# One-core graph layer with residual and layer norm: the last two batches' x weighed at the outset, pairs packed from the second batch on, three transpose banks, two units' x added on TensorE, new end orders

## Chip, core and metric

The kernel runs on one core of one Trainium2 chip. The metric is the device time of one execution in microseconds; lower is better. The profile is of one execution by the hardware profiler. Engines: PE is TensorE (PEld its weight loads), DVE VectorE, ACT ScalarE, POOL GpSimd, SP SyncE.

## What is computed

```python
masks = (relation[None] == rel_ids[:, None, None, None]).astype(x.dtype)  # adj == 1..4
h = jnp.einsum('rbnm,bmd->rbnd', masks, x)        # B=8, N=1024, D=128, R=4
y = jnp.einsum('rbnd,rdo->bno', h, weight) + bias
out = layernorm(x + y, axis=-1)
```

The adjacency matrices (int32, 4 MB for each of 8 batches) hold only 0 and 1 in the inputs, so only relation 1 contributes. The kernel computes for that case, checks on the chip that it holds and that x is in range, and has a second pass for any other input, which is not entered here.

## The kernel before

A *unit* is 128 rows of an adjacency matrix (u = 0 to 7 in a batch), a *pair* is two units (k = 0 to 3), numbered through as 4b + k, so the last is pair 31. A pair is one load of 1 MB (the units of batch 0 come alone, 512 KB each). Output rows are handled in *groups* of four units, two to a batch (numbers 0 to 13); the last batch has five, of 2, 2, 2, 1 and 1 units, called a, a2, c, e, d.

What happens to a pair:

- SP loads it (`load_adj`, L405). Three slots; a slot is loaded again when pair 4b + k - 12 was checked. SP's queue is one order written out by hand: the units of batch 0, x of batch 1, then for each batch its pairs and x of the next. The stores come after all loads. ACT's queue issues x of batches 0 and 7 and the bias at the start.
- ACT checks it (`check`, L532): one pass over the pair that also writes it as bytes, two units side by side in 16 bits.
- PE transposes it. Packed (from pair 8 on, `transpose_pair`, L644) both units go in 8 transposes of the checked bytes; unpacked (L635) each unit takes 8 from the raw words, and waits for no check. Four PSUM banks (`T_BANKS`) take turns.
- DVE makes a mask out of each unit (`mask_unit`, L836). In the last batch ACT makes the masks of units 5 and 7 (`mask_second`, L578).
- PE multiplies (`products`, L666): 16 matmuls of 256 columns for two units, with x as a high and a low fp16 part. After four units ACT copies the sum (`copy_h`, L549), PE multiplies by the weight (`project`, L678), DVE adds x and bias (`sum_rows`, L843), takes statistics (L849) and combines them (L860).

The last batch is done the other way round. Its x is multiplied by the weight at the outset (transposed L688, kept by DVE L816, weighed L697, split into z_hi and z_lo by ACT L570 and DVE L821). `rows_of_unit` (L718) then gives a unit's rows in 16 matmuls of 128 columns with no copy and no projection. For the very last unit d, PE adds x as well (`add_x`, L728), so that DVE needs no sum.

The roots of a batch: ACT takes a square root (`root`, L554), DVE offers its reciprocal (`offer_guess`, L870), POOL makes of it scale and shift in seven small steps (`roots`, L470 to L487) and normalises unit by unit (L498). POOL also splits x of batches 2 to 6 (L444, L450) and adds the bias to every x (`add_bias`, L459). At the end three sets remain: `full` (batch 6), `ra` (units 0 to 3 of batch 7), `rb` (units 4 to 7). POOL normalises four units of `full`, two of `ra` and one of `rb`, in this order; ACT has the others but two; DVE has the last two (L899), whose scale it works out itself (L875 to L894). SP stores each set.

```python
            full, ra, rb = sets[B - 2:]
            roots(full)
            normalise(full, full.units[:4])
            roots(ra)
            normalise(ra, ra.units[:2])
            normalise(rb, rb.units[:1])
```

Of the kernel before, what the change touches and what calls it, by code (L numbers as in the profile page):

```python
# [5 lines left out]
P = 128  # L6
# [44 lines left out]
def adj_resnorm_kernel(nc, x, adj, weight, bias, out):  # L51
# [8 lines left out]
    FIRST_PACKED = 8  # L60
    T_BANKS = 4
# [29 lines left out]
    LAST = len(groups) - 5  # L91

# [42 lines left out]
    def pairs_checked_by(g):  # L135

        first = [3, 5, 8, 10]
        if g.index < len(first):
            return first[g.index]
        return min(2 * g.index + 4, PAIRS * B - 2)  # L140

    ctx = ExitStack()
    with ctx:
# [30 lines left out]
        z_hi = sb("z_hi", [P, J, D], FP16)  # L174
        z_lo = sb("z_lo", [P, J, D], FP16)
# [4 lines left out]
        x_t = h_all[:, 2:4, :]  # L180
# [20 lines left out]
        y_ps = pb("y_ps", [P, GU, D], FP32)  # L201

# [5 lines left out]
        def y_of(g):  # L208

            if g.index < LAST:  # L210
                return y_ps
            if g.place < 2:
                return h_ps[g.place][:, :].rearrange("p (n d) -> p n d", d=D)
            if g.place == 2:
                return y_ps
            if g.place == 3:
                return ids_t[0][:, :, :].bitcast(FP32).rearrange("p j q -> p (j q)").rearrange("p (n d) -> p n d", d=D)
            return spare

        def half_of_z(half):  # L220

            return (spare[:, :, :], h_ps[1][:, :].rearrange("p (n d) -> p n d", d=D))[half]
# [24 lines left out]
        s_turned, s_kept = sem("halves_of_last_x_transposed"), sem("halves_of_last_x_t_kept")  # L247
# [35 lines left out]
        x_v, adj_v, out_v = (t.rearrange("b (k p) d -> b p k d", p=P) for t in (x, adj, out))  # L283

# [104 lines left out]
        def _(sp):  # L389
# [42 lines left out]
        def _(pool):  # L432
# [20 lines left out]
            def add_bias(b):  # L453

                if b == B - 1:
                    pool.wait_ge(s_turned, 2)
                else:
                    pool.wait_ge(s_lo, b + 1)
                nc.gpsimd.tensor_tensor(x_sb[:, b], x_sb[:, b],  # L459
                                        bias_sb[:, :].unsqueeze(1).to_broadcast([P, J, D]),  # L460
                                        ALU.add).then_inc(s_xb, 1)

# [40 lines left out]
            add_bias(0)  # L503
            for b in range(B - 1):
                if b + 1 < B - 1:
                    if b:
                        split_hi(b + 1)
                    split_lo(b + 1)
                add_bias(b + 1)
# [12 lines left out]
        def _(act):  # L522
# [24 lines left out]
            def copy_h(g):  # L547
                act.wait_ge(s_prod, g.index + 1)
                nc.scalar.activation(h_all[:, g.bank, 0:g.count * P], h_ps[g.bank][:, 0:g.count * P], ACT.Copy,  # L549
                                     scale=0.5).then_inc(s_h, 1)  # L550
# [17 lines left out]
            def split_z(half):  # L568
                act.wait_ge(s_z, half + 1)
                nc.scalar.activation(z_hi[:, half * HALF:(half + 1) * HALF], half_of_z(half), ACT.Copy,  # L570
                                     scale=0.5).then_inc(s_zh, 1)

            def mask_second(u):


                act.wait_ge(s_mask, unit_no(B - 1, u) if u < J - 1 else unit_no(B - 1, u) - 1)
# [5 lines left out]
            act.dma_start(bias_row[:, :], bias.rearrange("(a d) -> a d", a=1)).then_inc(s_bias, 16)  # L582
            act.preload_act_table(ACT.Sqrt)
# [7 lines left out]
            split_z(0)  # L591
            check(0, 2)
            split_z(1)
            for g in groups[1:LAST]:
                copy_h(groups[g.index - 1])
# [24 lines left out]
        def _(pe):  # L620
# [26 lines left out]
            def products(g, units, part):  # L647

                if part is x_hi:
# [5 lines left out]
                    if g.index == 1 and units[0] == g.first:  # L655

                        pe.wait_ge(s_zl, 2)
# [13 lines left out]
            def project(g):  # L671
                pe.wait_ge(s_h, g.index + 1)
                if g.index == 0:
                    pe.wait_ge(s_biased, 1)
# [8 lines left out]
            def transpose_last_x(half):  # L683
                if half == 0:
                    pe.wait_ge(s_whole, 1)
                    pe.wait_ge(s_x[B - 1], 16)
                for n in range(HALF):
                    last = nc.tensor.transpose(half_of_z(half)[:, n, :], x_sb[:, B - 1, half * HALF + n, :],  # L688
                                               whole_ident[:, :])
                last.then_inc(s_turned, 1)  # L690

            def weigh_last_x(half):
                pe.wait_ge(s_kept, half + 1)
                if half == 0:
                    pe.wait_ge(s_w, 16)
                for n in range(HALF):
                    last = nc.tensor.matmul(half_of_z(half)[:, n, :], x_t[:, half, n * P:(n + 1) * P], w_sb[:, 0, :],  # L697
# [3 lines left out]
            def rows_of_unit(g, u):  # L701
                if u == g.first and g.place < 2:

                    pe.wait_ge(s_h, LAST - 1 + g.place)
                if u == g.first and g.place == 2:

                    pe.wait_ge(s_sum, LAST)
                pe.wait_ge(s_zl, 2)
                if g.place < 2 or g.place == 2 and u == g.first:
                    pe.wait_ge(s_mask, unit_no(g.b, u) + 1)  # L710
                elif g.place == 3:

                    pe.wait_ge(s_mask, unit_no(g.b, u))
                else:
                    pe.wait_ge(s_high, 1 if g.place == 2 else 2)
                for j in range(J):
                    for part in (z_hi, z_lo):
                        last = nc.tensor.matmul(y_of(g)[:, u - g.first, :], mask_t[:, g.b % 2, j, u * P:(u + 1) * P],  # L718
                                                part[:, j, :], start=(j == 0 and part is z_hi and g.place < 4),
# [4 lines left out]
            def add_x(g):  # L724

                pe.wait_ge(s_zl, 2)
                pe.wait_ge(s_xb, g.b + 1)
# [9 lines left out]
            idle_turns(44, 1)  # L737
# [24 lines left out]

            def step_by_two(g, units, b, k):
                if packed(b, k):
                    transpose_pair(b, k)
                    for part in (x_hi, x_lo):
                        products(g, units, part)
                elif (b, k) == (1, 0):

                    products(g, units, x_hi)  # L770
                    transpose_unit(b, 2 * k)
                    products(g, units, x_lo)
                    transpose_unit(b, 2 * k + 1)
                else:
# [3 lines left out]
                    products(g, units, x_lo)  # L778

            for g in groups[1:LAST]:  # L780
# [23 lines left out]
        def _(dve):  # L804
# [9 lines left out]
            def keep_last_x(half):  # L814
                dve.wait_ge(s_turned, half + 1)
                nc.vector.tensor_copy(x_t[:, half, :].rearrange("p (n d) -> p n d", d=D), half_of_z(half)).then_inc(s_kept, 1)  # L816

            def split_z(half):
                dve.wait_ge(s_zh, half + 1)
                js = slice(half * HALF, (half + 1) * HALF)  # L820
                nc.vector.scalar_tensor_tensor(out=z_lo[:, js], in0=half_of_z(half), scalar=0.5, in1=z_hi[:, js],  # L821
                                               op0=ALU.mult, op1=ALU.subtract).then_inc(s_zl, 1)

            def row_maxima_of_z():
                dve.wait_ge(s_zh, 2)
                nc.vector.tensor_reduce(row_max[:, B - 1, :], z_hi[:, :, :], AX.X, ALU.max,
# [13 lines left out]
            def sum_rows(g):  # L840
                dve.wait_ge(s_y, g.index + 1)
                dve.wait_ge(s_xb, g.b + 1)
# [64 lines left out]
            def find_far():  # L907

                dve.wait_ge(s_rm, B - 1)
                dve.wait_ge(s_zm, 1)  # L910
# [28 lines left out]
            keep_last_x(0)  # L939
            keep_last_x(1)  # L940
            for u in range(2, GU + 1):
                mask_unit(0, u)
            split_z(0)
            row_maxima(0)
            mask_unit(0, GU + 1)
            split_z(1)

            for g in groups[1:LAST]:
# [5 lines left out]
                if g.place == 0:  # L954
                    row_maxima(g.b)
                elif g.b:
# [3 lines left out]
                sum_rows(q)  # L960
                mask_unit(n.b, n.units[0])
# [4 lines left out]
                if g.index == 2:  # L966
                    row_maxima_of_z()
# [29 lines left out]
            normalise(rb, e.first, rows[:, rb.b, e.first, :])  # L997
# [21 lines left out]
```

## Time and profile before

| what | before |
|---|---|
| time, median of 3 runs | 110.03 us (109.78 to 110.26) |
| the profiled execution | 109.81 us, of which the span from first to last instruction is 108.0 |
| busy | PE 92%, PEld 86%, DVE 78%, ACT 79%, POOL 68% |
| moved by DMA | 42.21 MB, 391 GB/s over the span |
| granted clock | 0.989 of full |

A row of a timeline gives the start, the duration, the engine, the line and the tiles; in brackets, how long the engine was idle before it and what released it. Matmul ends are modelled, so for PE the starts are the surer figures.

### The profile page before, as it was taken

The page shows a single profiled execution, that of the slowest core. Times are in us where ns is not written, and L with a number is a line of the kernel's source. Part 1 is how long each engine was busy: PE and PEld are TensorE (multiplying, and loading weights), DVE is VectorE, ACT ScalarE, POOL GpSimd, SP SyncE. Part 2 cuts the span into 40 slices and gives each one's busy share as a digit, 9 for nine tenths or more (in the row PEclk, how much of TensorE's full clock was granted, in tenths as well). Part 3 has the DMA queues.
Part 4 walks back from the last instruction along what each step waited for, and adds up shares of the span by engine and source line. Part 5 has one row for each costly group of instructions (what it writes and reads, how often), then busy time and mean ns, then how long its engine had stood idle before and what let it go on. Part 6 is the DMA issues. An engine that isn't in the chain of part 4 may idle for free.

```text
span 108.0 us, 3036 instructions
## 1 busy us (share of the span) xinstructions
PE 99.9 (92%) x1100; PEld 92.4 (86%) x1100; DVE 83.9 (78%) x251; ACT 85.4 (79%) x103; POOL 73.6 (68%) x137
## 2 busy tenths in 40 slices
PE   5979999998999999999999999999999999999800
PEld 5957998998999999889998999899998999999800
DVE  1035779357979999699979998889978997997880
ACT  1346977979969897899799979997899879895850
POOL 3000800096099799989998899989998994934870
PEclk9999999999999999999999999999999999999995
DMA  3999999999999999999999999999999999999145
GB/s 58 350 414 420 420 414 435 431 428 403 437 428 431 411 419 432 428 422 414 429 431 428 413 422 434 434 422 419 422 428 425 428 419 426 414 419 367 58 201 199
DMA packets 7793, 42.21 MB, mean 391 GB/s; under 512 B 865, under 2 KB 994, under 8 KB 4194
## 3 DMA queue, kind: packets, MB, share of 16 engines
q1 hardware_dynamic: 7488, 40.96, 91.6%
q10 hardware_dynamic: 290, 1.05, 2.5%
q8 instruction: 9, 0.15, 0.5%
q14 instruction: 6, 0.05, 0.1%
HBM read 37.81 MB, written 4.19 MB: 389 GB/s over the span
## 4 chain that ended last, share of the span: by engine, by line
DMA 52%; PE 33%; DVE 7%; ACT 4%; issue 1%; DVEq 0%
DMA adj_sb<-adj 52%; PE h_ps L666 14%; PE ids_t L635 5%; PE y_ps L678 4%; PE ids_t L644 3%; PE h_ps L718 3%; ACT bytes_of L532 2%; DVE mask_t L836 2%; DVE x_lo L904 1%; ACT mask_t L578 1%; PE h_ps L697 1%; PE spare L697 1%; DVE stats L849 1%; PE spare L688 1%; DVE x_sb L899 1%
## 5 line engine op out<-in xcount | busy, mean ns | idle before, releaser
L532 ACT ACTIVATE bytes_of<-adj_sb,offset 128x2048 fp8e4<-128x2048 int32 x32 | 64.1, 2003 | 4.3 <-DMA adj_sb<-adj 3.8
L836 DVE TENSOR_SCALAR mask_t<-ids_t 128x1024 uint16<-128x1024 uint16 x62 | 40.4, 683 | 13.1 <-PE ids_t L635 11.1
L666 PE MATMUL h_ps<-mask_t,x_hi 128*128 128x256 bf16 (+1 forms) x232 | 29.2, 269 | 1.0 <-DVE mask_t L836 0.9
L666 PE MATMUL h_ps<-mask_t,x_lo 128*128 128x256 bf16 (+1 forms) x232 | 29.4, 269 | 0.2 <-DVE x_lo L904 0.2
L459 POOL TENSOR_TENSOR x_sb<-x_sb,bias_sb 128x1024 f32<-128x1024 f32 x8 | 19.1, 2382 | 9.9 <-ACT bias_sb L589 9.5
L498 POOL TENSOR_SCALAR x_sb<-x_sb,rstd,shift 128x128 f32<-128x128 f32 x55 | 23.9, 455 | 1.4 <-DVE shift L894 0.5
L666 PEld LDWEIGHTS h_ps<-mask_t,x_lo 128*128 128x128 f16 x232 | 21.9, 98 | 2.8 <-DVE x_lo L904 0.4
L666 PEld LDWEIGHTS h_ps<-mask_t,x_hi 128*128 128x128 f16 x232 | 21.1, 98 | 3.4 <-DVE mask_t L836 1.3
L450 POOL TENSOR_TENSOR x_lo<-x_sb,x_hi 128x1024 f16<-128x1024 f32 x6 | 12.9, 2146 | 8.3 <-ACT x_hi L545 7.9
L644 PE MATMUL ids_t<-ident,bytes_of 128*128 128x128 bf16 x192 | 16.2, 227 | 0.1
L644 PEld LDWEIGHTS ids_t<-ident,bytes_of 128*128 128x128 bf16 x192 | 14.6, 148 | 1.5 <-ACT bytes_of L532 1.1
L678 PE MATMUL y_ps<-w_sb,h_all 128*128 128x128 f32 x112 | 14.9, 276 | 0.0
L549 ACT ACTIVATE h_all<-h_ps 128x512 f32<-128x512 f32 x14 | 8.4, 599 | 7.1 <-PE h_ps L666 6.8
L849 DVE BATCH_NORM_STATS2 stats<-x_sb 128x6 f32<-128x128 f32 x63 | 13.8, 280 | 0.1
L678 PEld LDWEIGHTS y_ps<-w_sb,h_all 128*128 128x128 f32 x112 | 13.6, 192 | 0.3
L843 DVE TENSOR_TENSOR x_sb<-y_ps,x_sb 128x512 f32<-128x512 f32 (+1 forms) x15 | 9.9, 660 | 2.2 <-PE y_ps L678 2.2
L635 PE MATMUL ids_t<-ident,adj_sb 128*128 128x128 bf16 x128 | 10.6, 228 | 0.2 <-DMA adj_sb<-adj 0.2
L635 PEld LDWEIGHTS ids_t<-ident,adj_sb 128*128 128x128 bf16 x128 | 9.9, 148 | 0.5 <-issue 0.4
L811 DVE TENSOR_REDUCE row_max<-x_hi 128x8 f32<-128x1024 f16 x7 | 8.5, 1210 | 0.0
L444 POOL CAST x_hi<-x_sb 128x1024 f16<-128x1024 f32 x5 | 5.2, 1042 | 3.7 <-DMA x_sb<-x 3.7
L733 PE MATMUL h_ps<-mask_t 128*128 128x128 bf16 (+2 forms) x46 | 5.5, 311 | 1.2 <-DVE mask_t L928 1.2
L532 ACT ACTIVATION_READ_ACCUMULATOR bytes_of<-adj_sb,offset 128x1 f32 x32 | 6.0, 187 | 0.0
(85 smaller groups left out, 84.1 us busy)
## 6 DMA issues: line engine op xcount, KB each, us to landing
adj_sb<-adj SPq DMA_DIRECT2D x28, 1024.0 KB, 24.3
adj_sb<-adj SPq DMA_DIRECT2D x8, 512.0 KB, 8.7
out<-x_sb SPq DMA_DIRECT2D x7, 512.0 KB, 21.7
x_sb<-x SPq DMA_DIRECT2D x6, 512.0 KB, 23.4
x_sb<-x ACTq DMA_DIRECT2D x2, 512.0 KB, 6.5
out<-x_sb SPq DMA_DIRECT2D x2, 256.0 KB, 2.1
w_sb<-weight SPq DMA_DIRECT2D x1, 64.0 KB, 5.9
bias_row<-bias ACTq DMA_DIRECT2D x1, 0.5 KB
```

The costliest lines, as they stand in the source:

```text
L450: nc.gpsimd.tensor_tensor(x_lo[:, b % 2], x_sb[:, b], x_hi[:, b % 2], ALU.subtract).then_inc(s_lo, 1)
L459: nc.gpsimd.tensor_tensor(x_sb[:, b], x_sb[:, b], bias_sb[:, :].unsqueeze(1).to_broadcast([P, J, D]), ALU.add).then_inc(s_xb, 1)
L498: last = nc.gpsimd.tensor_scalar(rows[:, slot, u, :], rows[:, slot, u, :], rstd[:, slot, u:u + 1], shift[:, slot, u:u + 1], ALU.mult, ALU.add)
L532: nc.scalar.activation(bytes_of[:, at % ROOM].rearrange("p n t -> p t n"), adj_sb[:, slot, 2 * k:2 * k + 2, :], ACT.Square, scale=SLOPE, b ...
L635: last = nc.tensor.transpose(bank[:, j, :], words[:, j // step(b), j % step(b), 0, :], ident[:, :])
L644: last = nc.tensor.transpose(bank[:, j, :], words[:, j // step(b), j % step(b), :], ident[:, :])
L666: last = nc.tensor.matmul(h_ps[g.bank][:, to], part[:, g.b % 2, j, :], mask_t[:, g.b % 2, j, cols], start=(j == 0 and part is x_hi), stop= ...
L678: last = nc.tensor.matmul(y_of(g)[:, n, :], h_all[:, g.bank, n * P:(n + 1) * P], w_sb[:, 0, :], start=True, stop=True)
L811: nc.vector.tensor_reduce(row_max[:, b, :], x_hi[:, b % 2], AX.X, ALU.max, apply_absolute_value=True).then_inc(s_rm, 1)
L836: nc.vector.tensor_scalar(mask_t[:, b % 2, :, u * P:(u + 1) * P].bitcast(UINT16), ids_t[bank_of(turn)][:, :, :].bitcast(UINT16), 1 << bit, ...
L843: nc.vector.tensor_tensor(rows[:, g.b, g.us, :], y_of(g)[:, 0:g.count, :], x_sb[:, g.b, g.us, :], ALU.add).then_inc(s_sum, 1)
L849: last = nc.vector.bn_stats(stats[:, u, :], rows[:, g.b, u, :])
```

## The change

Batch 6 joins batch 7: the x of both are weighed at the outset in four halves, with their bias added by POOL right then (`add_bias_late`); groups 12 and 13 are done by `rows_of_unit`. x of batch 6 is loaded by ACT's queue at the start and no longer by SP between batches 5 and 6. Pairs are packed from pair 4 on (the second batch). Three banks for transposes leave one for z and for e. PE adds x for e as for d. The turns that keep PE busy before the first data are 20 of 256 columns in place of 44 of 128. The orders at the end are new on ACT, PE and DVE; POOL's is as it was. In outline:

```diff
-    FIRST_PACKED = 8
-    T_BANKS = 4
+    FIRST_PACKED = 4
+    T_BANKS = 3
+    ROWS = LAST - 2
+    Z_BATCHES = (B - 1, B - 2)
 ...
-                    if k == PAIRS - 1 and b + 1 < B - 1:
+                    if k == PAIRS - 1 and b + 1 < B - 2:
                         load_x(b + 1)
 ...
             add_bias(0)
+            add_bias_late(0)
+            add_bias_late(1)
 ...
             act.dma_start(bias_row[:, :], bias.rearrange("(a d) -> a d", a=1)).then_inc(s_bias, 16)
+            act.dma_start(units_of(x_sb[:, B - 2], B - 2, 0, J), rows_of(x, B - 2, 0, J)).then_inc(s_x[B - 2], 16)
 ...
-            copy_h(groups[LAST - 1])
-            for k in (c.first // 2, e.first // 2):
-                check(a.b, k)
+            check(c.b, c.first // 2)
+            check(e.b, e.first // 2)
             root(full)
             mask_second(c.units[1])
             mask_second(d.first)
-            normalise(full, full.units[4:5])
             root(ra)
-            normalise(full, full.units[5:]).then_inc(s_aside, 1)
+            normalise(full, full.units[4:]).then_inc(s_aside, 1)
 ...
             pe.wait_ge(s_still, 1)
-            idle_turns(44, 1)
+            idle_turns(20, 2)
 ...
-            transpose_last_x(0)
-            transpose_last_x(1)
-            transpose_unit(0, 2)
+            transpose_half(0)
+            transpose_half(1)
             for part in (x_hi, x_lo):
                 products(g, g.units[1:2], part)
+            transpose_unit(0, 2)
+            weigh_half(0)
+            transpose_half(2)
+            transpose_half(3)
             transpose_unit(0, 3)
-            weigh_last_x(0)
+            weigh_half(1)
             transpose_unit(0, GU)
-            weigh_last_x(1)
             products(g, g.units[2:], x_hi)
+            weigh_half(2)
             transpose_unit(0, GU + 1)
             products(g, g.units[2:], x_lo)
+            weigh_half(3)
 ...
-            for g in groups[1:LAST]:
+            for g in groups[1:ROWS]:
                 n = groups[g.index + 1]
                 step_by_two(g, g.units[:2], g.b, g.units[2] // 2)
                 project(groups[g.index - 1])
                 step_by_two(g, g.units[2:], n.b, n.first // 2)
+            for g in groups[ROWS:LAST]:
+                n = groups[g.index + 1]
+                transpose_pair(g.b, g.units[2] // 2)
+                for u in g.units[:2]:
+                    rows_of_unit(g, u)
+                if g.index == ROWS:
+                    project(groups[g.index - 1])
+                transpose_pair(n.b, n.first // 2)
+                for u in g.units[2:]:
+                    rows_of_unit(g, u)
             a, a2, c, e, d = groups[LAST:]
+            add_x(e)
             add_x(d)
             transpose_pair(a2.b, a2.first // 2)
-            project(groups[LAST - 1])
 ...
             before = groups[LAST - 1]
+            sum_rows(before)
             mask_unit(a2.b, a2.units[0])
             mask_unit(a2.b, a2.units[1])
-            sum_rows(before)
             statistics(before)
             combine(r, before, r.units)
+            sum_rows(a)
             mask_unit(c.b, c.units[0])
-            sum_rows(a)
             statistics(a)
-            offer_guess(r)
             mask_unit(e.b, e.first)
             sum_rows(a2)
+            offer_guess(r)
             statistics(a2)
             combine(ra, a2, ra.units)
             sum_rows(c)
-            offer_guess(ra)
             statistics(c)
             combine(rb, c, c.units)
-            sum_rows(e)
-            statistics(e)
+            offer_guess(ra)
+            statistics_of_sum(e)
             combine(rb, e, e.units)
```

In DVE's loop the row maxima of batch 6 (in group 12) go, and those of its z are taken in group 5; in ACT's loop `copy_h` ends with group 11, since groups 12 and 13 need none.

## Rows read from the trace of the kernel before

**Rows 1.** The page: bandwidth in 40 equal slices of the span.
```profile
GB/s 58 350 414 420 420 414 435 431 428 403 437 428 431 411 419 432 428 422 414 429 431 428 413 422 434 434 422 419 422 428 425 428 419 426 414 419 367 58 201 199
```

**Rows 2.** Windows: start and engines, then granted clock, DMA share, GB/s.
```profile
0.00:4.00 4.00, 2.81 (x27) 2.82 (x28) 0.43 (x6) 1.28 (x1) 0.97 (x7) 1.00 0.51 137
4.00:10.00 6.00, 5.01 (x55) 4.12 (x53) 1.91 (x4) 2.20 (x3) 0.00 (x0) 1.00 1.02 410
67.00:78.10 11.10, 11.10 (x115) 10.12 (x114) 9.71 (x29) 9.70 (x12) 10.40 (x18) 1.00 1.02 425
```

**Rows 3.** Timeline of ACT: checks of pairs 23, 24, 25 and 31.
```profile
73.02 2.01 ACT L532 ACTIVATE bytes_of<-adj_sb,offset 128x2048 fp8e4<-128x2048 int32 x1 [0.17 <-DMA adj_sb<-adj]
...
76.68 2.00 ACT L532 ACTIVATE bytes_of<-adj_sb,offset 128x2048 fp8e4<-128x2048 int32 x1 [0.22 <-DMA adj_sb<-adj]
...
79.19 2.01 ACT L532 ACTIVATE bytes_of<-adj_sb,offset 128x2048 fp8e4<-128x2048 int32 x1 [0.22 <-DMA adj_sb<-adj]
...
94.83 2.00 ACT L532 ACTIVATE bytes_of<-adj_sb,offset 128x2048 fp8e4<-128x2048 int32 x1
```

**Rows 4.** Timeline of PE: transposes of pairs 8, 21, 25 and 31.
```profile
34.86 0.66 PE L644 MATMUL ids_t<-ident,bytes_of 128*128 128x128 bf16 x8
...
70.23 0.71 PE L644 MATMUL ids_t<-ident,bytes_of 128*128 128x128 bf16 x8
...
81.34 0.71 PE L644 MATMUL ids_t<-ident,bytes_of 128*128 128x128 bf16 x8
...
98.07 0.66 PE L644 MATMUL ids_t<-ident,bytes_of 128*128 128x128 bf16 x8
```

**Rows 5.** Chain of waits in order of time: start, duration, what.
```profile
10.36 0.59 PE spare L688 x4
...
13.27 0.95 PE spare L697 x8
...
86.94 0.49 PE ids_t L644 x8
87.43 1.75 PE h_ps L666 x16
89.18 0.89 PE y_ps L678 x8
...
92.32 0.22 PE spare L728 x2
...
94.16 1.79 PE h_ps L718 x32
```

**Rows 6.** Timeline of DVE: a sum, offers of guesses, a mask, last statistics.
```profile
84.73 0.69 DVE L843 TENSOR_TENSOR x_sb<-y_ps,x_sb 128x512 f32<-128x512 f32 x1 [0.23 <-PE y_ps L678]
...
89.78 0.20 DVE L870 RECIPROCAL first_guess<-std 128x8 f32<-128x8 f32 x1 [0.53 <-ACT std L554]
...
97.95 0.18 DVE L870 RECIPROCAL first_guess<-std 128x8 f32<-128x8 f32 x1
98.77 0.69 DVE L836 TENSOR_SCALAR mask_t<-ids_t 128x1024 uint16<-128x1024 uint16 x1 [0.64 <-PE ids_t L644]
99.38 0.41 DVE L843 TENSOR_TENSOR x_sb<-h_ps,x_sb 128x256 f32<-128x256 f32 x1
...
102.69 0.27 DVE L855 BATCH_NORM_STATS2 stats<-spare 128x6 f32<-128x128 f32 x1
...
105.02 0.41 DVE L899 TENSOR_SCALAR x_sb<-spare,moments,rstd 128x128 f32<-128x128 f32 x1
```

**Rows 7.** Timeline of POOL: from the guess for batch 6 to its last row.
```profile
98.28 0.20 POOL L475 TENSOR_TENSOR product<-sixteenth,first_guess 128x8 f32<-128x8 f32 x1 [1.13 <-DVE first_guess L870]
...
103.55 0.89 POOL L498 TENSOR_SCALAR x_sb<-x_sb,rstd,shift 128x128 f32<-128x128 f32 x2
104.94 0.48 POOL L498 TENSOR_SCALAR x_sb<-x_sb,rstd,shift 128x128 f32<-128x128 f32 x1 [0.50 <-DVE shift L894]
```

**Rows 8.** Groups by line and shape: the idle turns before the first data.
```profile
L733 PE MATMUL h_ps<-mask_t 128*128 128x128 bf16 x44 | 4.9, 310 | 1.2 <-DVE mask_t L928 1.2
```

More of the change, by code:

```diff
@@ L201, in adj_resnorm_kernel @@
         y_ps = pb("y_ps", [P, GU, D], FP32)
+        other = pb("other", [P, GU, D], FP32)
         spare = pb("spare", [P, GU, D], FP32)
@@ L208, in y_of, with rows_bank, z_of @@
         def y_of(g):
+            if g.index < ROWS:
+                return y_ps
             if g.index < LAST:
[L211 to L218, printed above, removed]
+                return rows_bank(g.place)
+            return (y_ps, rows_bank(0), rows_bank(1), other, spare)[g.place]
+        def rows_bank(n):
+            return h_ps[n][:, :].rearrange("p (n d) -> p n d", d=D)
         def half_of_z(half):
-            return (spare[:, :, :], h_ps[1][:, :].rearrange("p (n d) -> p n d", d=D))[half]
+            return (rows_bank(1), spare[:, :, :], y_ps[:, :, :], other[:, :, :])[half]
+        def z_of(part, half):
+            b, js = Z_BATCHES[half // 2], slice(half % 2 * HALF, (half % 2 + 1) * HALF)
+            return part[:, b - (B - 2), js]
         s_w = sem("weights_loaded")
@@ L591, in _ @@
             split_z(0)
+            split_z(1)
             check(0, 2)
-            split_z(1)
+            split_z(2)
+            check(0, 3)
             for g in groups[1:LAST]:
-                copy_h(groups[g.index - 1])
+                if g.index <= ROWS:
+                    copy_h(groups[g.index - 1])
+                if g.index == 1:
+                    split_z(3)
                 for n, at in enumerate(range(pairs_checked_by(groups[g.index - 1]), pairs_checked_by(g))):
@@ L680, in project, with transpose_half, weigh_half @@
                 last.then_inc(s_y, 1)
[L683 to L686, printed above, removed]
+            def transpose_half(half):
+                b, first = Z_BATCHES[half // 2], half % 2 * HALF
+                pe.wait_ge(s_whole, 1)
+                pe.wait_ge(s_x[b], 16)
+                if half == 2:
+                    pe.wait_ge(s_biased, 1)
                 for n in range(HALF):
-                    last = nc.tensor.transpose(half_of_z(half)[:, n, :], x_sb[:, B - 1, half * HALF + n, :],
-                                               whole_ident[:, :])
+                    last = nc.tensor.transpose(half_of_z(half)[:, n, :], x_sb[:, b, first + n, :], whole_ident[:, :])
                 last.then_inc(s_turned, 1)
-            def weigh_last_x(half):
+            def weigh_half(half):
                 pe.wait_ge(s_kept, half + 1)
-                if half == 0:
-                    pe.wait_ge(s_w, 16)
+                pe.wait_ge(s_w, 16)
                 for n in range(HALF):
-                    last = nc.tensor.matmul(half_of_z(half)[:, n, :], x_t[:, half, n * P:(n + 1) * P], w_sb[:, 0, :],
+                    last = nc.tensor.matmul(half_of_z(half)[:, n, :], x_t[half][:, n * P:(n + 1) * P], w_sb[:, 0, :],
                                             start=True, stop=True)
@@ L718, in rows_of_unit @@
                         last = nc.tensor.matmul(y_of(g)[:, u - g.first, :], mask_t[:, g.b % 2, j, u * P:(u + 1) * P],
-                                                part[:, j, :], start=(j == 0 and part is z_hi and g.place < 4),
+                                                part[:, g.b - (B - 2), j, :],
+                                                start=(j == 0 and part is z_hi and g.place < 3),
                                                 stop=(j == J - 1 and part is z_lo))
@@ L778, in step_by_two @@
                     products(g, units, x_lo)
-            for g in groups[1:LAST]:
+                elif pair_no(b, k) < FIRST_PACKED + 2:
+                    products(g, units, x_hi)
+                    transpose_pair(b, k)
+                    products(g, units, x_lo)
+                else:
+                    transpose_pair(b, k)
+                    for part in (x_hi, x_lo):
+                        products(g, units, part)
+            for g in groups[1:ROWS]:
                 n = groups[g.index + 1]
@@ L938, in _ @@
             mask_unit(0, 1)
[L939 to L942, printed above, removed]
+            keep_half(0)
+            keep_half(1)
+            mask_unit(0, 2)
+            keep_half(2)
+            keep_half(3)
+            mask_unit(0, 3)
             split_z(0)
-            row_maxima(0)
+            mask_unit(0, GU)
+            split_z(1)
             mask_unit(0, GU + 1)
-            split_z(1)
+            split_z(2)
             for g in groups[1:LAST]:
@@ L996, in _ @@
                 part(rb)
-            normalise(rb, e.first, rows[:, rb.b, e.first, :])
+            normalise(rb, e.first, y_of(e)[:, 0, :])
             normalise(rb, d.first, y_of(d)[:, 0, :]).then_inc(s_done, 1)
```

108 lines of the change are left out of this document (56 added, 52 removed).

## The prediction

> **What bounds the kernel now.** I read the page first. Bandwidth stands at some 420 GB/s from the second slice to the 36th and then collapses [rows 1], so most of the span is one saturated stream of loads. The windows say the same: in a stretch of 11.1 us, which is one batch, DMA is busy all the time at 425 GB/s, and PE is busy throughout too [rows 2]. One batch of loads is 4 x 1.049 MB and 0.524 MB of x, 4.72 MB, which at 425 GB/s is 11.1 us.
>
> The chain's pieces give PE's work for such a batch: four transposes of a pair at 0.50, four times two units' products at 1.75, two projections at 0.89 [rows 5], together 10.8 us. So DMA paces PE by a margin of 0.3 us a batch. ACT's checks show it: pairs 23, 24 and 25 each wait for DMA, and 23 and 24 stand 3.66 us apart against 2.51 for 24 and 25, because x of batch 6 lies between them [rows 3]. After pair 25 no x is loaded, pairs come faster than PE takes them, and PE runs without a stop from pair 25 at 81.34 over pair 31 at 98.07 [rows 4] to the last unit at 102.1. The check of pair 31 starts at 94.83 with no wait [rows 3], so the last load was there already.
>
> Then the tail. DVE takes d's statistics at 102.69 and normalises d until 105.43 [rows 6]; POOL makes its last row from 104.94 to 105.42 after having waited 0.50 for the scale [rows 7]. Both end together. A store, and the span ends at 108.0; another 1.8 us lies outside the span.
>
> **Part 1: the start.** Two more halves of x are transposed, 0.55 to 0.59 each, and two more weighed, 0.95 each [rows 5]: 3.0 us of PE. Packing batch 1 saves four times 0.50, 2.0 us. So pair 8, transposed at 34.86 before [rows 4], comes at about 36.0. x of batch 6 is now loaded ahead of nearly all pairs, so 0.524 MB at 425 GB/s [rows 2] puts off every load up to pair 23 by 1.24 us. PE's own lateness of 1.1 is therefore hidden under DMA's; PE's work alone would bring it to pair 24 at 36.0 + 4 x 10.8 = 79.2, and DMA lets it there later, as follows. Pair 4 now needs its check, ACT has two more splits, and DVE two more copies and two more splits; what that costs in batch 1 has, with 10.8 against 11.1, four batches to be made up. I cost it at nothing; bounds 0 and, if PE stands 2 us more at the start, 2 - 0.9 = 1.1 at pair 24.
>
> **Part 2: where the stream stands at pair 21 to 25.** All reads together are the same bytes, so pairs 24 to 31 land as before, but pair 21 lands 1.24 later. PE transposed it at 70.23, now 71.47. From there to pair 25 before took 11.11 us [rows 4] with PE's work of 10.8, which is now no longer stretched by the x between pairs 23 and 24. Pair 25: 71.47 + 10.8 = 82.3, 0.95 us later than before. Bounds: 0 (the stream had 49% of its engines free in the first 4 us [rows 2], and if x of batch 6 fits in there nothing moves) and 0.95. The loads that precede it on ACT's queue are x of 0 and 7, and from 4 us on the share is full, so I take 0.95.
>
> **Part 3: the rows of batch 6.** Two units' rows cost 1.79 against 1.75 for their products [rows 5]; what goes is the projection of groups 12 and 13. From pair 25 to pair 31 PE now has six transposes (3.0), twelve units of rows (12 x 0.895 = 10.74), project of group 11 (0.89) and two `add_x` of 0.22: 15.1 us, against 16.73 before [rows 4]. Pair 31 is transposed at 82.3 + 15.1 = 97.4, 0.7 earlier than 98.07. The check can't limit this: pair 31 is loaded as before, and ACT, without the last two copies of h, has it checked by 96.
>
> **Part 4: DVE, and the guess for batch 6.** Here the new order matters. POOL can't start the roots of `full` before DVE's `offer_guess(full)`. Before it stood right behind the statistics of a, at 97.95 [rows 6], ahead of the mask of e. Now it stands behind the mask of e and the sum of a2. PE's side: the mask of e can't start before 0.70 after pair 31's transpose (98.07 to 98.77 [rows 4, 6]), the next instruction follows 0.60 later (98.77 to 99.38), then the sum of 0.41 [rows 6]: 97.4 + 0.70 + 0.60 + 0.40 = 99.1. DVE's side: from the sum of group 11 at 84.73 to that offer at 97.95 were 13.22 us, 0.53 of them a wait [rows 6]; the new order adds a mask (0.60) and a sum (0.40), 13.7. The sum of group 11 follows the projection, which ends 0.50 + 1.79 + 0.89 after pair 25's transpose, with 0.2 to start: 85.7. That gives 99.4. I take 99.3, 1.35 us later than before. The row maxima of batch 6 went ahead of that sum and only open a gap there.
>
> Masks: that of c's first unit comes from DVE at about 97.85, when PE wants it; ACT's mask of unit 5 is about 0.25 late for PE. So PE ends near 101.7, 0.4 earlier than before, and e needs no sum.
>
> **Part 5: the tail.** POOL's order has not changed. From the guess to the product is 0.33; from the product to the rows of `ra` 98.28 to 103.55, 5.27; two rows 0.89, and the row of `rb` follows directly, 0.46 [rows 6, 7]. Together 6.95: 99.3 + 6.95 = 106.25, against 105.42. ACT's rows of `ra` and its row of `rb` hang on the same shift and end there too. DVE meanwhile has d's statistics at 101.95 and, by the 2.74 us from there to the end of d [rows 6], is done at 104.7. The tail used to have DVE and POOL level; now POOL comes last, by 1.5 us. The 0.50 of slack that POOL had is used up, and the saved projections are not worth the later guess.
>
> **Sum** on the profiled execution: 109.81 + (106.25 - 105.42) = 110.6. That execution lies 0.22 under the median of 110.03, so as a median 110.8 us. The last two stores now follow each other by less than half a microsecond where it was one: 0 to 0.2 more, in the range.
>
> **The start's clock.** The 44 idle turns of 128 columns took 4.9 us [rows 8], 0.11 each, twice the 0.056 of a row matmul of 128 columns (1.79 over 32 [rows 5]): the lower level, 1.2 GHz, though the window's column gives 1.00. 20 turns of 256 are 4.3 us by the same rate, so PE stands idle for about 0.7 us more before the first unit lands. The Trainium skill, "TensorE: Matmul & The Clock Gate", Part 1, says that the clock is at its low level by default and rises when the engine has been at work. By that rule the lift could come later, and by the row alone at the same time; no trace of before can show which. As a mechanism: some 3 us of PE work in the first data at twice its time would put pair 8 at 38 to 39, of which 0.9 is absorbed by pair 24 (79.2 against 80.1): up to 1.1 us on all that follows, 111.9 us at most, 111.4 likely.
>
> **Rivals.**
> - *The late guess costs 0.3 to 1.2 us (as summed).* For it: the orders as written, and rows of either engine. 110.8 us, own range 110.3 to 111.3. Chance 0.52.
> - *The stream does not shift, or half of it.* Pair 25 then comes up to 0.95 earlier, the guess at 98.3 to 98.9, the end between 0.2 earlier and 0.4 later: 109.8 to 110.4. For it: the half-idle DMA of the first 4 us. Against: only a part of that is free at the time x of batch 6 is issued. Chance 0.23.
> - *DVE's chain sets the end, faster than before.* If the whole stream runs 1.3 us ahead because the idle DMA of the first 4 us is filled, and PE takes pair 26 before 84.1, the guess is out before 97.9 and POOL no longer late; the end then is d's, 104.7, 0.7 earlier: 109.3 us. It decides at a guess before 98.0. Against: PE's own work from pair 8 on does not allow pair 25 before 81.4. Chance 0.10.
> - *The clock rises later or the first batches are late on ACT and DVE:* 111.4. Chance 0.15.
>
> **How the numbers follow.** About 0.5% (0.55 us) is what a measurement of this kernel can tell from none. Slower by more: the clock's 0.15 and two thirds of the first, 0.35, and a little of the second, 0.51 in all. Within: the rest of the first and most of the second, 0.36. Faster: 0.13. The range takes in the second rival and most of the fourth: 109.7 to 111.5.
>
> **What would show it.** Right: POOL's last rows follow one another without a wait and end after DVE's, at about 106.2; the offer of batch 6's guess starts near 99.3; pair 23's check starts at about 74.3 and pair 25's at 79.2; pair 31 is transposed near 97.4; PE's last unit near 101.7. Wrong: POOL still waits for the last shift; pair 23 at 73.0; the guess before 98.5; idle turns followed by products of 256 columns at 0.21 each, which is the lower clock.

## The result, and the profile after

The changed kernel takes 112.58 us (median of 4 runs, 112.00 to 112.91) against 110.01; the ratio is 1.0235, 95% interval 1.0210 to 1.0259. That is 2.6 us slower, where 0.8 was forecast, and outside the range. The profiled execution took 112.82 us with a span of 110.9, against 109.81 and 108.0.

The page's bandwidth slices say where not to look: the stream is as full as in [rows 1] up to the 36th slice.
```profile
GB/s 50 359 420 420 421 422 440 419 425 422 420 425 425 422 428 417 425 427 420 427 422 424 427 425 422 428 428 428 414 425 428 419 424 418 408 384 74 191 191 9
```
ACT's timeline shows the checks of pairs 21, 23 and 25:
```profile
69.42 2.01 ACT L548 ACTIVATE bytes_of<-adj_sb,offset 128x2048 fp8e4<-128x2048 int32 x1 [0.22 <-DMA adj_sb<-adj]
...
74.27 2.01 ACT L548 ACTIVATE bytes_of<-adj_sb,offset 128x2048 fp8e4<-128x2048 int32 x1
...
79.88 2.00 ACT L548 ACTIVATE bytes_of<-adj_sb,offset 128x2048 fp8e4<-128x2048 int32 x1
```
and PE's the transposes of pairs 25 and 31, which answer to [rows 4]:
```profile
82.38 0.66 PE L667 MATMUL ids_t<-ident,bytes_of 128*128 128x128 bf16 x8
...
97.52 0.66 PE L667 MATMUL ids_t<-ident,bytes_of 128*128 128x128 bf16 x8
```
Forecast were 74.3 for the check of pair 23 (74.27), 82.3 for the transpose of pair 25 and 97.4 for that of pair 31. The check of pair 25 was forecast for 79.2 and starts at 79.88, without a wait for DMA: the loads no longer set its time, and since pair 25 is transposed where the sum had it, nothing hangs on the miss. DVE's timeline, to set beside [rows 6]: the offer of batch 6's guess, d's statistics, d's last step, and the flag for the second pass:
```profile
99.16 0.20 DVE L912 RECIPROCAL first_guess<-std 128x8 f32<-128x8 f32 x1
...
101.80 0.30 DVE L897 BATCH_NORM_STATS2 stats<-spare 128x6 f32<-128x128 f32 x1
...
104.41 0.40 DVE L941 TENSOR_SCALAR x_sb<-spare,moments,rstd 128x128 f32<-128x128 f32 x1
104.73 0.13 DVE L1048 CAST again<-ids_t 1x1 int32<-1x1 f32 x1
```
POOL's, beside [rows 7]: the last three rows follow one another with no wait.
```profile
99.51 0.20 POOL L489 TENSOR_TENSOR product<-sixteenth,first_guess 128x8 f32<-128x8 f32 x1 [2.19 <-DVE first_guess L912]
...
104.76 1.31 POOL L512 TENSOR_SCALAR x_sb<-x_sb,rstd,shift 128x128 f32<-128x128 f32 x3
```
The guess was forecast for 99.3 and starts at 99.16; POOL's end for 106.25 and is at 106.07; DVE's for 104.7 and is at 104.81. Up to the last computed row the sum holds within 0.2 us, and that row is 0.65 later than before. Yet the span grew by 2.9. What is left lies behind the last computed row. Asked for the last store alone (`out` on SP's queue, from 106 on), the trace answers:
```profile
L417 SPq DMA_DIRECT2D out<-x_sb x1: 372/372/372, 106.1 to 106.1; - x1
...
DMA to landing us min/median/max: 4.3/4.3/4.3
```
In the trace of before, the flag and the same store read:
```profile
105.34 0.14 DVE L1000 CAST again<-ids_t 1x1 int32<-1x1 f32 x1
...
L408 SPq DMA_DIRECT2D out<-x_sb x1: 332/332/332, 105.5 to 105.5; - x1
...
DMA to landing us min/median/max: 2.0/2.0/2.0
```
So 2.9 = 0.6 of later issue + 2.3 of slower landing. The DMA queues in the three windows 107 to 108, 108 to 109 and 109 to 110 us (packets, MB, share of 16 engines) show how:
```profile
q1 hardware_dynamic: 181, 0.31, 81.6%
q8 instruction: 1, 0.02, 8.6%
...
q14 instruction: 1, 0.01, 3.0%
q1 hardware_dynamic: 1, 0.00, 1.4%
...
q1 hardware_dynamic: 8, 0.01, 5.3%
```
q1 carries the loads and stores. Nearly all packets of the last two stores are through by 108; 9 more, about one engine's share, trickle in until 109.9. One packet of an instruction queue stands among them: 8.6% of 16 engines in one microsecond is 1.4 us of one engine. (The trace does not name the engine of a packet; that it is one and the same is inferred from these amounts and times.) In windows of 0.2 us it starts in 107.4 to 107.6, and the first straggler of q1 moves in 108.8 to 109.0, 1.4 us later. Before, the same packet comes at 107.4, when the last store's packets are through. The windows 107.0 to 107.2 and 107.4 to 107.6 of that trace have:
```profile
q1 hardware_dynamic: 14, 0.01, 11.0%
...
q8 instruction: 1, 0.02, 32.5%
```

This gave the theory for the experiments. When DVE has handed out the flag, all engines branch over the code of the second pass; some 2.1 to 2.8 us after the flag (both ends seen: before and the changed kernel), code is fetched by DMA. Before, POOL and DVE ended together, the last store went out 0.15 us behind the flag, and its packets were ahead of the fetch. The late guess makes POOL end 1.3 us after DVE, so the store goes out 1.4 us behind the flag and meets the fetch on one engine. Rivals: the last two stores are too close (0.43 us apart, 1.0 before), or the late store is slow for its own sake.

The Trainium skill, "DMA: Bandwidth & Descriptors", in the section on queues, rings and completion order, says that a DMA engine takes turns between queues and changes only behind a whole packet. The 1.4 us that the stragglers wait for one packet agrees with it.

### The profile page after: what moved, and what is told of

Read it like the earlier page. It is cut to its first block, busy times and chain, and to the rows that moved or that the text cites. A ratio compares the mean times of both kernels' runs of the same rounds, so it can differ in the third digit from the quotient of the medians.

```text
span 110.9 us, 3073 instructions
## 1 busy us (share of the span) xinstructions
PE 99.1 (89%) x1118; PEld 91.6 (83%) x1118; DVE 85.2 (77%) x254; ACT 84.5 (76%) x103; POOL 70.1 (63%) x135
## 4 chain that ended last, share of the span: by engine, by line
PE 52%; DMA 27%; ACT 6%; POOL 5%; DVE 2%; issue 2%; SPq 1%; POOLq 0%; DVEq 0%
DMA adj_sb<-adj 27%; PE h_ps L689 19%; PE h_ps L743 8%; PE ids_t L667 8%; ACT bytes_of L548 6%; PE y_ps L702 5%; PE ids_t L658 4%; POOL x_sb L512 3%; DVE mask_t L875 2%; PE y_ps L743 2%; SPq L414 1%; PE spare L722 1%; PE h_ps L722 1%; PE y_ps L722 1%; PE other L722 1%
## 5 line engine op out<-in xcount | busy, mean ns | idle before, releaser
L689 PE MATMUL h_ps<-mask_t,x_hi 128*128 128x256 bf16 (+1 forms) x200 | 25.5, 272 | 0.9 <-DVE mask_t L875 0.9
L689 PE MATMUL h_ps<-mask_t,x_lo 128*128 128x256 bf16 (+1 forms) x200 | 25.5, 272 | 0.0
L689 PEld LDWEIGHTS h_ps<-mask_t,x_hi 128*128 128x128 f16 x200 | 18.3, 100 | 3.5 <-DVE mask_t L875 1.7
L465 POOL TENSOR_TENSOR x_sb<-x_sb,bias_sb 128x1024 f32<-128x1024 f32 x6 | 14.3, 2380 | 10.7 <-ACT bias_sb L609 10.3
L667 PEld LDWEIGHTS ids_t<-ident,bytes_of 128*128 128x128 bf16 x224 | 17.2, 148 | 0.7 <-ACT bytes_of L548 0.5
L743 PE MATMUL h_ps<-z_hi,mask_t 128*128 128x128 f16 x96 | 11.4, 220 | 0.0
L743 PE MATMUL h_ps<-z_lo,mask_t 128*128 128x128 f16 x96 | 11.4, 220 | 0.0
L743 PEld LDWEIGHTS h_ps<-z_hi,mask_t 128*128 128x128 bf16 x96 | 9.4, 98 | 0.0
L743 PEld LDWEIGHTS h_ps<-z_lo,mask_t 128*128 128x128 bf16 x96 | 9.4, 98 | 0.0
L759 PE MATMUL h_ps<-mask_t 128*128 128x256 bf16 (+1 forms) x22 | 5.5, 430 | 1.2 <-DVE mask_t L970 1.2
```

The costliest lines, as they stand in the source:

```text
L465: nc.gpsimd.tensor_tensor(x_sb[:, b], x_sb[:, b], bias_sb[:, :].unsqueeze(1).to_broadcast([P, J, D]), ALU.add).then_inc(s_xb, 1)
L667: last = nc.tensor.transpose(bank[:, j, :], words[:, j // step(b), j % step(b), :], ident[:, :])
L689: last = nc.tensor.matmul(h_ps[g.bank][:, to], part[:, g.b % 2, j, :], mask_t[:, g.b % 2, j, cols], start=(j == 0 and part is x_hi), stop= ...
```

## Experiments: the tail

Each kernel was timed side by side with the kernel before, and the ratio is to that; intervals are 95%.

**The guess moved forward.** The only edit to the changed kernel:
```diff
             statistics(a)
+            offer_guess(r)
             mask_unit(e.b, e.first)
             sum_rows(a2)
-            offer_guess(r)
```


> The changed kernel with DVE's offer of batch 6's guess back behind the statistics of a, ahead of the mask of e. Late-guess theory: the guess starts near 98.0 in place of 99.16, POOL's last row ends about 0.7 to 0.9 us earlier than 106.07, when it again waits for or just meets the last shift. If the two last stores' closeness is what makes the second land 4.3 us after its issue, they are still less than 0.6 us apart and the landing stays at 4: time 0.8 under the changed kernel's 112.6, 111.8. If the long landing comes from its meeting other traffic at a fixed moment after the end of the check for a second pass, it changes too, and the time comes to 109.5 to 110.5. If the guess has no part: 112.6.

Measured: 109.14 us, ratio 0.9967 (0.9951 to 0.9982). One line moved takes off 2.7% and makes the kernel 0.3% faster than before, which is small but clear of the interval. The same kernel was run again later, as the measure for three of the runs below:

> The kernel with only the guess moved forward in the change, a second time and in five rounds, as the measure for the other three: 109.1 to 109.3, 0.3 to 0.5% under the kernel before.

Measured: 109.55, ratio 0.9954 (0.9940 to 0.9968). In its trace the guess starts at 97.82, 1.34 earlier:
```profile
97.82 0.18 DVE L912 RECIPROCAL first_guess<-std 128x8 f32<-128x8 f32 x1
...
104.68 0.14 DVE L1048 CAST again<-ids_t 1x1 int32<-1x1 f32 x1
```
and POOL ends with DVE:
```profile
103.40 1.32 POOL L512 TENSOR_SCALAR x_sb<-x_sb,rstd,shift 128x128 f32<-128x128 f32 x3
```
The last store is issued at 104.8 and lands after 2.1, though the last two stores are 0.5 us apart. The flag stands at 104.68, where it stood in the changed kernel; of the two, only the store has moved.

**No branch.** The branch on the flag is left out on all engines, and with it the second pass: the fallback for inputs out of range is missing.
```diff
             engine.wait_ge(s_again, 1)
-            with engine.If(engine.value_load(again[0:1, 0:1], min_val=0, max_val=P) > 0):
-                ...
```


> The changed kernel with the branch over the second pass left out on all five engines (they still wait for the flag): the fallback for inputs outside the range is gone. Fetch theory: packets of the instruction queues, which the page shows in the last microseconds (1.4 us of one DMA engine at 107 to 108), sit ahead of the last store's packets on one engine; without a jump they go, the last store lands 2.0 to 2.4 us after its issue in place of 4.3, and the time is some 2 us lower, 110.5. Close-stores theory: the landing stays at 4.3 and the time at 112.6 less some 0.3 for the missing code.

Measured: 110.26, ratio 1.0059 (1.0042 to 1.0076), 1.8% under the changed kernel's ratio. The order at the end is that of the changed kernel and the last store is issued at 105.8, but it lands as it did before:
```profile
L411 SPq DMA_DIRECT2D out<-x_sb x1: 372/372/372, 105.8 to 105.8; - x1
...
DMA to landing us min/median/max: 2.2/2.2/2.2
```
and its trace has no packet of an instruction queue after 103.4. That speaks for the fetch and against closeness: the stores are as close as they were (105.4 and 105.8).

**The late guess alone, in the kernel before.** The same edit the other way round.
```diff
             statistics(a)
-            offer_guess(r)
             mask_unit(e.b, e.first)
             sum_rows(a2)
+            offer_guess(r)
```


> The kernel before with the offer of batch 6's guess behind the mask of e and the sum of a2, as the change has it. Late-guess theory: the guess goes from 97.95 to about 99.9 (it now waits for the sum of a2), POOL's last row ends at about 106.9, 1.4 us later, with the last two stores under half a microsecond apart. Close-stores theory: the last store then lands 4 us after its issue, time 110.0 + 1.4 + 2.2 = 113.6. If closeness is harmless: 111.4. If the guess's place costs nothing: 110.0.

Measured: 111.22, ratio 1.0144 (1.0127 to 1.0161): the case in which closeness does no harm. The guess starts at 99.66 and the last row of POOL ends at 106.69, 1.27 later than before. Here DVE is late as well, since it still sums e, so the flag comes at 106.26, the store goes out 0.45 behind it, and it lands after 2.2. So the late guess by itself costs 1.6 us, and no collision comes with it. The margin is thin: the fetch comes in the window 108.4 to 108.6, where the store's last packets also are.

**One store for the last batch.**
```diff
-            engine.wait_ge(s_last, 16 * len(sets[B - 1:]))
+            engine.wait_ge(s_last, 16)
...
             for r in sets:
+                if r.index == B - 1:
+                    continue
+                if r.index == B:
+                    r = Rows(B - 1, 0, J, B)
```


> The changed kernel with the two last stores joined into one of 512 KB, issued when all rows of batch 7 are done. Close-stores theory: no second store runs behind a first, it lands 2.6 to 3.4 us after its issue as the 512 KB store of batch 6 did, the time is about 112.6 - 1.5 = 111.1. Fetch theory: the packets still meet the fetch, landing 4.3 or later, 112.6 or more.

Measured: 112.38, ratio 1.0243 (1.0216 to 1.0271), no gain. A single store of 512 KB, issued at 105.8, lands after 4.4. With a single store there is none that it could follow too closely: closeness is out.

**The flag held back**, until POOL is through.
```diff
+            dve.wait_ge(s_norm, B + 1)
             dve.wait_ge(s_count, 1)
             nc.vector.tensor_copy(again[:, :], ids_t[1][0:1, 0, 0:2].bitcast(FP32)).then_inc(s_again, 1)
```


> The changed kernel; DVE hands out the flag for the second pass only when POOL's last row is done (106.1 in place of 104.9), so all engines' branches come after the last store's issue. Fetch theory: the fetch of code follows the flag by 2.1 to 2.7 us, so it comes at 108.3 or later, when the last store's packets are through; that store lands 2.2 us after its issue, not 4.3; SP's own branch is 1.3 us late and hides most of this under the store: 110.4 to 110.8. A theory in which the last store is slow for its own sake, or the branch merely costs time: landing 4.3, time 112.6 or more.

Measured: six of eight runs at 110.10 to 110.85 (ratio 1.0054, 1.0030 to 1.0077), two at 112.3 to 112.5. The trace is of one of the latter two: the flag is at 107.95, the last store at 107.9, it lands after 2.2, and the fetch comes at 110.4. So with all branches kept, holding them back wins back most of what the collision cost; that it does so in the six shorter runs is shown by their times alone, since none of them has a trace. Why two runs are 2 us longer is another matter, shown below.

**The flag brought forward, in the kernel before.** The converse: nothing is late, only the flag is early.
```diff
-            for part in (invert, times_guess, times_guess_again, better_guess, shift_last):
+            for part in (invert, times_guess, times_guess_again):
+                part(rb)
+            dve.wait_ge(s_count, 1)
+            nc.vector.tensor_copy(again[:, :], ids_t[1][0:1, 0, 0:2].bitcast(FP32)).then_inc(s_again, 1)
+            for part in (better_guess, shift_last):
                 part(rb)
...
             normalise(rb, d.first, y_of(d)[:, 0, :]).then_inc(s_done, 1)
-            dve.wait_ge(s_count, 1)
-            nc.vector.tensor_copy(again[:, :], ids_t[1][0:1, 0, 0:2].bitcast(FP32)).then_inc(s_again, 1)
```


> The kernel before, with the flag handed out some 0.8 us earlier, between two of DVE's last small steps, while the last store goes out 0.1 us later. Nothing else moves. Fetch theory: the fetch of code, at the flag plus 2.1 to 2.7 us, now meets the packets of the last store, at its issue plus 1.1 to 1.7, which lands about 4 us after its issue: 111.5 to 112. Otherwise: 109.7 and a landing of 2.0.

Measured: three runs at 111.97 to 112.17 and one at 109.51, so no ratio is given. The granted clock does not set the three (0.980 to 0.986) apart from the short one (0.986); in the executions of the kernel before beside them it was 0.983 to 0.998. The last store of the profiled run, at 105.6:
```profile
L408 SPq DMA_DIRECT2D out<-x_sb x1: 332/332/332, 105.6 to 105.6; - x1
...
DMA to landing us min/median/max: 4.0/4.0/4.0
```
and its queues in the windows 106 to 107, 107 to 108 and 108 to 109 show the fetch and then the stragglers:
```profile
q1 hardware_dynamic: 132, 0.24, 61.5%
q8 instruction: 1, 0.02, 9.7%
...
q1 hardware_dynamic: 39, 0.05, 13.4%
q14 instruction: 1, 0.01, 2.9%
...
q1 hardware_dynamic: 6, 0.01, 5.5%
```
This makes the collision out of nothing else: 2 us in the kernel before, for a flag that is 0.8 us early. The same early flag gave one run at 109.51, and it has no trace; that the fetch missed the store there is likely and not shown.

The traces side by side (us; the packet's time is that of its window of 0.2; the last column is the time from issue to landing):

| kernel | flag | last store issued | q8 packet | landing |
|---|---|---|---|---|
| before | 105.34 | 105.5 | 107.4 | 2.0 |
| changed | 104.73 | 106.1 | 107.4 | 4.3 |
| guess early (second measurement) | 104.68 | 104.8 | 107.2 | 2.1 |
| no branch | - | 105.8 | none | 2.2 |
| before, guess late | 106.26 | 106.7 | 108.4 | 2.2 |
| one last store | 104.45 | 105.8 | 106.6 | 4.4 |
| flag late | 107.95 | 107.9 | 110.4 | 2.2 |
| before, flag early | 104.50 | 105.6 | 106.6 | 4.0 |

The landing is slow in the three where the store goes out 1.1 to 1.4 us after the flag, and in no other. The six traces that are not in the table (the guess early in its first measurement, batch 6's x at the start, 44 and 10 idle turns, batch 1 unpacked, x of e on DVE) have the last store 0.1 to 0.5 us behind the flag, and it lands after 2.0 to 2.2.

## Experiments: the start

**Batch 6's x loaded early, in the kernel before.** Only the load moves; nothing is weighed early.
```diff
-                    if k == PAIRS - 1 and b + 1 < B - 1:
+                    if k == PAIRS - 1 and b + 1 < B - 2:
...
+            act.dma_start(units_of(x_sb[:, B - 2], B - 2, 0, J), rows_of(x, B - 2, 0, J)).then_inc(s_x[B - 2], 16)
             act.preload_act_table(ACT.Sqrt)
```


> The kernel before; only x of batch 6 is loaded by ACT's queue at the start and no longer between batches 5 and 6. Theory of the prediction (part 2): pairs up to 23 land 1.24 us later, PE reaches pair 25 at 82.3 in place of 81.34 and everything after is 0.95 later: 110.5 to 110.9. If the half-idle DMA of the first 4 us takes it in: 109.7 and the check of pair 23 at 73.0.

Measured: 110.97, ratio 1.0087 (1.0074 to 1.0100), 0.93 us for a forecast of 0.95. Its transpose of pair 25 is 1.17 later than in [rows 4]; 0.14 of that may be the first unit, transposed at 6.41 in this run and at 6.27 before:
```profile
82.51 0.66 PE L645 MATMUL ids_t<-ident,bytes_of 128*128 128x128 bf16 x8
```

**44 idle turns again.**
```diff
-            idle_turns(20, 2)
+            idle_turns(44, 1)
```


> The changed kernel with the guess early (109.14 in its first run) and 44 idle turns of 128 columns as before. In the trace of the changed kernel the first transposes and products run at the lower clock until about 9.9 and PE's first unit is done 0.9 us later than before. Theory that this is absorbed by waiting for DMA up to pair 20: same time, 109.1 within 0.2, with pair 12 and later pairs at the same starts. Rival, that it carries through: 108.4.

Measured: 109.32, ratio 0.9945 (0.9925 to 0.9966), not distinguishable from the 0.9967 and 0.9954 with 20 turns. At the start PE was late in the changed kernel; its timeline has
```profile
8.20 1.04 PE L689 MATMUL h_ps<-mask_t,x_hi 128*128 128x128 bf16 x8 [0.36 <-DVE mask_t L875]
...
36.55 0.66 PE L667 MATMUL ids_t<-ident,bytes_of 128*128 128x128 bf16 x8
```
Eight matmuls of 128 columns in 1.04 us are the lower clock, though the granted clock in the window's row is 1.00 in both kernels. Those of the kernel before took 0.62:
```profile
7.84 0.62 PE L666 MATMUL h_ps<-mask_t,x_hi 128*128 128x128 bf16 x8 [0.57 <-DVE mask_t L836]
```
By pair 25 nothing of it is left: with 44 turns it is transposed at 82.67 after a first unit at 6.58, with 20 turns and the guess early at 82.27 after a first unit at 6.35.

**Ten idle turns.**
```diff
-            idle_turns(20, 2)
+            idle_turns(10, 2)
```


> Guess early, with 10 idle turns of 256 columns in place of 20. PE then idles from 3.3 to about 6. Theory that the level of the clock in the first batch decides (a run of the kernel with the late flag stood at the lower level at 10 us, had pair 8 at 38.9 in place of 36.6 and pair 31 at 99.4 in place of 97.1): the same here in every run, 2 us slower, 111.0 to 111.6, with a branch that may meet the last store or not. Rival, that PE's lateness in the first batch is hidden under the loads whatever its size: 109.2.

Measured: three runs at 109.60 to 109.89 (ratio 0.9977, 0.9960 to 0.9994) and one at 111.94, which has no trace and a granted clock of 0.994: what made it long is open. The expected 2 us are wrong. PE was idle for 3.2 us ahead of the first unit and ran at the lower clock until about 11, but pair 31 is transposed at 97.76, 0.3 later than with 20 turns (97.44), and its first unit came 0.35 later (6.70 for 6.35). That is the rival: lateness of this size is hidden.

What made the traced one of the two long runs of the held-back flag long is told by its trace; the other is like it in time and granted clock (0.955 and 0.956 over the span). The windows of 4 to 10 and 10 to 20 us show the granted clock at 0.90 and 0.72:
```profile
4.00:10.00 6.00, 4.27 (x35) 2.65 (x33) 1.89 (x3) 1.15 (x2) 0.00 (x0) 0.90 1.02 412
10.00:20.00 10.00, 10.00 (x86) 9.50 (x87) 5.33 (x9) 5.63 (x8) 6.76 (x3) 0.72 1.03 426
```
After the first unit, at the upper level, the clock fell to the lower at about 9 and came back at about 15.5 (the window 9 to 15 has 0.50). Pair 8 was transposed at 38.86, 2.3 later than in the changed kernel's trace, and pair 31 at 99.37, 1.9 later. One run of the last kernel below (110.97, clock 0.960) looks like it, without a trace. The Trainium skill, "TensorE: Matmul & The Clock Gate", Part 1, has the clock lowered in idleness; before it fell PE had worked with gaps of 1.09 and 0.57 us, no more than with 44 turns (1.16 and 0.57), where it did not fall. What decides is left open.

**Batch 1 unpacked.**
```diff
-    FIRST_PACKED = 4
+    FIRST_PACKED = 8
```
(The order in which the first two packed pairs are taken moves with it, from pairs 4 and 5 to 8 and 9.)


> The changed kernel with the guess early, pairs of batch 1 unpacked. PE has 2.0 us more to do in batch 1, pair 8 comes at some 38.5 in place of 36.6. PE makes up 0.3 us a batch against DMA: by pair 24 it is 38.5 + 43.1 = 81.6 in place of 80.1, 1.5 us late, and that goes straight to the end: 110.4 to 110.8. If packing gains nothing here: 109.1.

Measured: 110.16 (109.70 to 110.81 in ten runs), ratio 1.0027 (1.0004 to 1.0050), 0.8 us over the 109.32 (0.9945) measured beside it with 44 idle turns; against the two measurements with 20 turns (0.9967 and 0.9954) it is 0.6 to 0.7%, 0.7 to 0.8 us. The forecast of 110.4 to 110.8 was too high. Pair 8 is transposed at 38.56, as expected, and pair 31 at 98.97 against 97.44, but this trace is of the longest of the ten runs. Packing is what lets PE bear the extra x of the start.

**x of e added by DVE again.**
```diff
-                                                start=(j == 0 and part is z_hi and g.place < 3),
+                                                start=(j == 0 and part is z_hi and g.place < 4),
...
-            add_x(e)
...
-            statistics_of_sum(e)
+            sum_rows(e)
+            statistics(e)
...
-            normalise(rb, e.first, y_of(e)[:, 0, :])
+            normalise(rb, e.first, rows[:, rb.b, e.first, :])
```


> Guess early, and x of unit e added by DVE again: PE has 0.22 us less before pair 29, DVE a sum of 0.26 and its wait more between e and d. In the trace with the guess early DVE's last row and POOL's end within 0.1 us of each other. Theory: DVE's last steps start at d's statistics, 0.2 to 0.4 later, and PE's 0.22 earlier takes half of it back: 0 to 0.3 us slower than with x of e on PE. Rival: no difference within 0.1.

Measured: 109.39, 109.68, 109.71 and 110.97, ratio 0.9992 (0.9947 to 1.0038). The median is 0.14 above the kernel with x of e on PE measured beside it (109.55), and the interval holds no difference too: inconclusive.

## Why the prediction was wrong

- **Part 1, the start.** Right in the main. Pair 8 comes at 36.55 for a forecast of 36.0, and the lateness is hidden by pair 25.
- **Part 2, the shift of the stream.** Right, and shown alone: 0.95 forecast, 0.93 measured. Only the check of pair 25 stood 0.7 later than forecast, at no cost.
- **Part 3, rows of batch 6.** Right by the trace: from pair 25 to pair 31 were 15.14 us, 15.1 forecast. Not tried by itself.
- **Part 4, the guess.** Right: 99.16 for 99.3. The deciding line was the one named.
- **Part 5, the tail.** Right in POOL and DVE, and right that POOL comes last by 1.3 us (1.5 forecast). The size that the late guess has alone is 1.6 us in the kernel before.
- **The sum.** This is the step that failed. It took what follows the last computed row as it was, "0 to 0.2 more" for the two stores following each other closely. It was 2.3 more. Closeness does account for up to 0.2 of it (landing 2.1 to 2.2 for 2.0 where no fetch interferes), as the prediction had it; the other 2.1 is the fetch of code for the branch, which [rows 1] to [rows 8] do not show but the trace of before did, as one packet at 107.4 just behind the last store. The jump over the second pass, which every execution makes, was treated as free. The signs named for a right prediction came out but for the check of pair 25, and none of them looked past the last computed row.
- **The clock.** The rival was half right: the rise did come later, at about 10 in place of 6, but it cost nothing that the run with 44 turns can tell.
- **The direction** (slower) and the mechanism of the likeliest case were right, its size was 0.8 for a measured 2.6. In the profiled executions it is 3.0: 0.65 from POOL's later end, 2.1 from the fetch, 0.2 from the close stores. The medians differ by 0.4 less, since the profiled execution lay 0.2 over the median in the changed kernel and 0.2 under it before. The run without the branch, which takes off 1.8%, or 1.9 us, agrees.
- **What the change is worth without its one line:** 0.3 to 0.5% faster than before. Of that, the early load costs 0.9 us and packing batch 1 gives 0.8; the rest is put down to the projections and copies saved and the shorter end, but no run tried these apart, so this is not shown.

## To carry to other kernels

At the end of a kernel follow every queue up to the last landing, the instruction queues as well: here a jump over code that never runs left the last store's landing at 2.0 to 2.2 us where the fetch came behind its packets, and cost 2 us where the fetch came while they were still waiting. When an order is rearranged so that one engine ends sooner, look at who waits for what it used to hand over early; here a reciprocal of 0.2 us, put behind a mask and a sum, held up POOL's whole chain. Extra work at a start that DMA paces is free up to what the pace leaves over, and what exceeds it shows at the end: 2.0 us more of PE work in batch 1 moved pair 31 by 1.5.

## Not expected of the hardware

- One packet of an instruction queue (0.02 MB) took 1.4 to 1.6 us beside stores in the three traces with a slow landing (1.0 before, with the engines idle), and the eight store packets behind it then took about 1.0 us, where a whole store of 256 KB moves in 0.8 us.
- The granted clock of the window's row stays 1.00 at a start where matmuls take the time of the lower level; a fall in mid-start is shown by it (0.72).
- The first unit of 512 KB was transposed, straight after it landed, between 5.86 and 6.70 us in different runs of nearly the same start, and what follows moves with it: with the guess early, pair 25 came at 81.94 in the run with 5.86 and at 82.27 in the one with 6.35.
